# A decoder layer on one core: the delta rule's loop over 64 units written out, five 32 x 32 block transposes on VectorE in each unit in place of PE products, and 24 products of the output projection in the last slot

## The reference

```python
mixed = silu(causal_conv1d(hidden @ w_qkv, conv_w))        # 4 taps
q, k, v = split(mixed)                                     # q, k normalised per head
beta, g = sigmoid(hidden @ w_b), -exp(A_log) * softplus(hidden @ w_a + dt_bias)
def step(St, inp):                                         # for each of 512 tokens
    q_t, k_t, v_t, g_t, b_t = inp
    St = St * exp(g_t)
    delta = (v_t - einsum('bhk,bhkv->bhv', k_t, St)) * b_t
    St = St + k_t[..., None] * delta[:, :, None, :]
    return St, einsum('bhk,bhkv->bhv', q_t, St)
core = rms_norm(core) * norm_weight * silu(hidden @ w_z)
return core.reshape(B, S, 4096) @ w_out                    # 32 heads x 128 -> 512
```

## Time and profile before

| what | us |
|---|---|
| median of 3 runs | 3666.68 |
| the profiled execution | 3667.28 |
| its span, first to last instruction | 3665.5 |
| `delta_rule`, first projection to last `o_turn` | 105.6 to 2802.4 |
| first product of the output projection | 2820.8 |

### The profile page before, as it was taken

One profiled execution on the slowest core, in us unless ns is written; L12 is line 12 of the kernel. 1 busy time (PEld: TensorE's weight loads), 2 busy tenths in 40 slices (PEclk: granted clock), 3 DMA queues, 4 the chain that ended last, 5 costly groups with the idle time before them and its releaser, 6 DMA issues. The chain is left out here.

```text
span 3665.5 us, 67720 instructions
## 1 busy us (share of the span) xinstructions
PE 3487.7 (95%) x23472; PEld 2207.6 (60%) x23472; DVE 2314.8 (63%) x4006; ACT 1369.4 (37%) x4187; POOL 1520.7 (41%) x1473
## 2 busy tenths in 40 slices
PE   4799999999999999999999999999996999999999
PEld 4466666666666666666666666666664444455444
DVE  4587777877778777878778777778772000014453
ACT  1344444444444444444444444444441000011232
POOL 0455554555545455555554555545551000001032
PEclk7999999999999999999999999999997999999999
DMA  1111111111111111111121111111104232311001
GB/s 55 44 36 30 42 42 37 30 36 44 34 36 30 36 32 51 30 36 36 31 48 30 36 30 41 43 37 30 36 24 157 87 115 69 103 58 69 1 9 38
DMA packets 94404, 165.88 MB, mean 45 GB/s; under 512 B 7841, under 2 KB 40737, under 8 KB 92449
## 3 DMA queue, kind: packets, MB, share of 16 engines
q1 hardware_dynamic: 93440, 152.47, 14.4%
q10 hardware_dynamic: 576, 8.39, 0.6%
HBM read 122.83 MB, written 38.01 MB: 44 GB/s over the span
## 5 line engine op out<-in xcount | busy, mean ns | idle before, releaser
L618 PE MATMUL d_ring<-xT,d_w 128*128 128x512 f32 x3072 | 1424.5, 607 | 12.0 <-DMA d_w<-in_w 11.6
L618 PEld LDWEIGHTS d_ring<-xT,d_w 128*128 128x128 f32 x3072 | 574.7, 194 | 585.6 <-issue 567.2
L890 DVE SCALAR_TENSOR_TENSOR d_conv<-d_ring,d_w,d_conv 128x511 f32<-128x511 f32 (+2 forms) x768 | 570.7, 743 | 287.2 <-ACT d_conv L1082 282.4
L1384 PE MATMUL t_acc<-t_area 128*128 128x512 f32 x1024 | 444.8, 595 | 18.4 <-DMA t_area<-core_rows 18.4
L1082 ACT ACTIVATE d_conv<-d_ring,d_w 128x512 f32<-128x512 f32 x256 | 176.5, 689 | 599.3 <-PE d_ring L618 599.3
L1384 PEld LDWEIGHTS t_acc<-t_area 128*128 128x128 f32 x1024 | 194.5, 191 | 256.7 <-issue 237.9
L923 DVE TENSOR_TENSOR d_zm<-d_tz,cons 128x512 f16<-128x512 f32 x384 | 264.2, 688 | 118.9 <-PE d_tz L688 114.5
L559 POOL TENSOR_TENSOR d_imd<-cons,d_dm 128x512 f16<-128x512 f32 x128 | 148.4, 1160 | 434.5 <-ACT d_dm L1133 434.5
L1613 DVE TENSOR_TENSOR t_x<-t_acc,t_x 128x512 f32<-128x512 f32 x16 | 11.1, 692 | 419.5 <-PE t_acc L1384 419.5
L511 POOL TENSOR_TENSOR d_rkt<-d_kss,cons 128x4 f32<-128x4 f32 x64 | 12.9, 201 | 610.9 <-ACT d_junk L1100 610.9
L933 DVE TENSOR_TENSOR d_em<-d_te,d_em 128x512 f16<-128x512 f32 x384 | 262.1, 683 | 4.5 <-PE d_td L697 0.2
(11 more groups left out here) (223 smaller groups left out, 6791.1 us busy)
## 6 DMA issues: line engine op xcount, KB each, us to landing
d_decay<-decay_rows SPq DMA_DIRECT2D x64, 512.0 KB, 6.1
core_rows<-d_core SPq DMA_DIRECT2D x64, 512.0 KB, 3.3
t_area<-core_rows SPq DMA_DIRECT2D x32, 1024.0 KB, 5.5
d_w<-in_w SPq DMA_DIRECT2D x96, 256.0 KB, 2.8
t_area<-in_wout ACTq DMA_DIRECT2D x2, 3072.0 KB, 21.3
ln_x<-in_x SPq DMA_DIRECT2D x16, 256.0 KB, 5.1
t_x<-in_x SPq DMA_DIRECT2D x4, 1024.0 KB, 9.9
t_area<-in_ctx SPq DMA_DIRECT2D x4, 1024.0 KB, 7.5
```

Of the source, the lines that this page charges most:

```text
L618: last = nc.tensor.matmul(bank(TILE[j])[:, :], wtile(j, k), xT[:, k, r % B * S:(r % B + 1) * S], start=k == 0, stop=k == KT - 1)
L890: nc.vector.scalar_tensor_tensor(c[:, d:S], bank(TILE[j])[:, 0:S - d], tap(j, KS - 1 - d), c[:, d:S], ALU.mult, ALU.add).then_inc(taps, 1)
L1384: return nc.tensor.matmul(acc[t][:, :], core[(grp * CHUNKS + q) % 3][:, t, h * P:(h + 1) * P], w[:, head, :], start=head == 0, stop=head = ...
```

## The change

1. **No loop.** `slots` and SP's list write all 66 slots out, and every count to wait for is a constant.
2. **Block transposes on VectorE.** `turn_e0`, `copy_d0` and the levels 0 to 3 of `level_e` go. As the matrices of those levels are block diagonal in blocks of at most 32, `flip_e0` makes the first `dm` and `flip_d` makes `em` after levels 0 to 3, each by one DVE transpose of 128x1024 fp16 in 32 x 32 blocks: 5 in a slot. Levels 4 and 5 keep their `level_e`.
3. **Work between engines.** `normal_k` goes from DVE to ACT (4 pieces of 128x128). `kq` is copied to SBUF by ACT (`copy_kq`) and multiplied by POOL (`p_full`, 2 a slot), no longer by DVE (L916). `first_state` and `first_output` (L952, L964) go from DVE to ACT. The order of all four lists and the ring's bank plan are new, and v0 comes before v1.
4. **Early products.** The ring and `td` use the four accumulators of the output projection, which now outlive `delta_rule`, as `xT` does. In `delta_rule` SP loads two `core` chunks and two weight chunks of 1 MB each into `xT` once the projections no longer need it. 24 of the 32 products of heads 0 to 7 and sequence 0 stand among the recurrence of the last slot (`head_start`), and 8 at the start of `tail`. `tail` begins its loads with chunk 2, and each piece of weights but the first waits for a chunk of `core`.

The core of the diff; the lists of the slots are shown by rows further down:

```diff
         def slots(eng, slot):
-            for r in range(ROUND):
-                slot((0, r), True, r >= 1, r >= 2)
-            with eng.Fori(1, ROUNDS, 1) as q:
-                for r in range(ROUND):
-                    slot((q, r), True, True, True)
-            slot((ROUNDS, 0), False, True, True)
-            slot((ROUNDS, 1), False, False, True)
+            for u in range(ITERS + 2):
+                slot((u // ROUND, u % ROUND), u < ITERS, 1 <= u <= ITERS, u >= 2)
...
+            sp.wait_ge(z_projected, GV * (ITERS - 1))
+            sp.wait_ge(stored, 16 * (ITERS - 4))
+            for q, b in ((0, 1), (1, 0)):
+                sp.dma_start(xT[:, :, b * S:(b + 1) * S], core_rows[0:NC, :, q * S:(q + 1) * S].rearrange("t p n -> p t n")).then_inc(early[0], 16)
+            sp.dma_start(xT[:, :, 2 * S:3 * S], wout[:, 0:KT, :]).then_inc(early[0], 16)
             slot((ROUNDS, 0), False, True, True)
+            sp.wait_ge(z_projected, GV * ITERS)
+            sp.dma_start(xT[:, :, 3 * S:4 * S], wout[:, KT:2 * KT, :]).then_inc(early[1], 16)
...
+            def p_full(m, h):
+                pool.wait_ge(kqs_ready, count(m))
+                pool.wait_ge(gamc_ready, nth(m, "gamc_ready", h))
+                nc.gpsimd.tensor_tensor(pT[m[1] % 2][h][:, :], kqs[:, :], gamc[m[1] % 2][h][:, :], ALU.mult).then_inc(p_ready, 1)
...
-            def turn_e0(m, h):
...
-                for c in range(NC):
-                    last = nc.tensor.matmul(chunk((tz, td)[h], c), piece(em[m[1] % 2], h, c), id16[:, :], start=True, stop=True)
...
+            def head_start(n, i):
+                if isinstance(n[0], int) and n == (ROUNDS, 1):
+                    if i == 0:
+                        pe.wait_ge(early[0], 48)
...
+                    for piece in range(EARLY * i // 19, EARLY * (i + 1) // 19):
+                        if piece == 4 * KT:
+                            pe.wait_ge(early[1], 16)
+                        early_product(nc, acc, xT, piece)
...
+            def flip_e0(m):
+                dve.wait_ge(e0_ready, at(m, 2 * GV, 2 * GV))
+                nc.vector.transpose(dm[:, :], em[m[1] % 2][:, :]).then_inc(flipped, 1)
+
+            def flip_d(m, l):
+                dve.wait_ge(d_added, at(m, 4, l + 1))
+                nc.vector.transpose(em[m[1] % 2][:, :], dm[:, :]).then_inc(flipped, 1)
...
+            def normal_k(n):
+                act.wait_ge(k_turned, count(n))
+                act.wait_ge(rk_ready, at(n, 2, 2))
...
+                for c in range(NC):
+                    nc.scalar.activation(chunk(khat[n[1] % 2], c), chunk(bank("k_turn"), c), ACT.Copy, scale=rk[:, c:c + 1]).then_inc(khat_ready, 1)
+
+            def copy_kq(m):
+                act.wait_ge(kq_done, count(m))
+                wait(act, p_ready, at(back(m, 1), GV, GV))
+                nc.scalar.activation(kqs[:, :], bank("kq")[:, :], ACT.Copy).then_inc(kqs_ready, 1)
...
+            for piece in range(EARLY, 8 * KT):
+                early_product(nc, acc, xT, piece)
             for grp in range(B):
-                for q in range(CHUNKS - 2):
+                for q in range(0 if grp else 2, CHUNKS - 2):
                     out_chunk(grp, q)
...
-        PARTS = (0, 2, 8, 20, HV)
+        PARTS = (8, 12, 16, 24, HV)
...
             for i in range(4):
+                if i:
+                    act.wait_ge(core_loaded[i - 1], 16)
                 act.dma_start(w[:, PARTS[i]:PARTS[i + 1], :], a["wout"][:, PARTS[i]:PARTS[i + 1], :]).then_inc(w_loaded[i], 16)
```

More of the change, by code:

```diff
@@ L424, in conv_of, with free @@
             return cb[CONV_BUFFER[name]]
-        def free(eng, n, name, order, place, freed):
-            slot_, v = back(n, -(name in LAGGED)), order.index(name)
+        def free(eng, n, name, order, place, freed, lag):
+            slot_, v = back(n, -lag[name]), order.index(name)
             for _ in range(3 * len(order)):
@@ L871, in slot @@
                 if recur:
+                    solve(s, 3)
+                    head_start(n, 15)
+                if invert:
+                    level_z(m, 5)
+                    v_turn(m, 1)
+                if recur:
+                    attend(s, 3)
+                    head_start(n, 16)
+                if invert:
+                    level_d(m, 5)
+                    level_e(m, 5)
+                if project:
+                    tile(n, 3)
+                if invert:
+                    refine(m, 1)
+                    refine(m, 0)
+                    tile(m, 4)
+                    close(m, 0)
+                if recur:
+                    o_turn(s, 0)
+                    head_start(n, 17)
                     o_turn(s, 1)
+                    head_start(n, 18)
                 if invert:
-                    close(m, 0)
                     close(m, 1)
+                    v_turn(m, 0)
             slots(pe, slot)
@@ L1227, with early_product, early_weights, tail @@
 A_X, A_H, A_HH, A_RES = (10752, 11776, 12800, 26624), 16384, (0, 2560, 5120, 18432), 20992
-def tail(nc, a, cons):
+def early_product(nc, acc, xT, piece):
+    head, t = piece // 4, piece % 4
+    core = xT[:, t, (1 - head // 4) * S + head % 4 * P:(1 - head // 4) * S + (head % 4 + 1) * P]
+    return nc.tensor.matmul(acc[t][:, :], core, early_weights(xT, head), start=head == 0, stop=False)
+def early_weights(xT, head):
+    return xT[:, head % 4, (2 + head // 4) * S:(3 + head // 4) * S]
+def tail(nc, a, cons, xT, acc, early):
     with ExitStack() as ctx:
@@ L1383, in project_out @@
                 head = q * 4 + h
-                return nc.tensor.matmul(acc[t][:, :], core[(grp * CHUNKS + q) % 3][:, t, h * P:(h + 1) * P], w[:, head, :],
+                rhs = early_weights(xT, head) if head < 2 * KT else w[:, head, :]
+                return nc.tensor.matmul(acc[t][:, :], core[(grp * CHUNKS + q - 2) % 3][:, t, h * P:(h + 1) * P], rhs,
                                         start=head == 0, stop=head == HV - 1)
@@ L1926, in decoder_layer @@
             gate_tables(nc, xT, tabs, cons, a["wab"], a["dt"], a["alog"], a["decay_rows"])
-            delta_rule(nc, xT, tabs, cons, nw, a["decay"], a["w"], a["core"])
-        tail(nc, a, cons)
+            acc = [outer.enter_context(nc.psum_tensor(f"acc{i}", [P, S], F32)) for i in range(4)]
+            delta_rule(nc, xT, tabs, cons, nw, acc, early, a["decay"], a["w"], a["core"], a["core_rows"], a["wout"])
+        tail(nc, a, cons, xT, acc, early)
 def lay_out(i):
```

477 lines of the change are left out of this document (232 added, 245 removed).

## The result

| | before | changed |
|---|---|---|
| median of the runs, us | 3667.24 (3666.51 to 3670.01, 4 runs) | 3456.73 (3456.25 to 3459.3, 4 runs) |
| ratio, 95% interval | 1 | 0.9426 (0.941 to 0.9442) |
| span of the profiled execution, us | 3665.5 | 3455.3 |

The kernel is 210.5 us faster where I had forecast 188.

A forecast was written before the change was run, and what follows sets the result against it. PE's issue of products was taken as the bound: 3665.5 - 86 (products) - 85.6 (loop) - 24 (end) + 8 (handoffs) = 3478 us of span, forecast 3479 us. Its own range was 3460 to 3505, the wider range 3455 to 3535.

The forecast's parts named there:

- What bounds it: In straight slots PE's issue of products is the bound, busy in all of 40.13 us; everything else is hidden.
- The slot: Four levels of e and two turns leave PE, 1.36 us in each of 63 slots: 86 us gained.
- The handoffs: Late answers stall PE at z and d of levels 1, 4 and 5: 0.12 us a slot, 8 us lost.
- VectorE: Five transposes a slot at 1.2 us each; DVE at 32.4 us, POOL 24.9, ACT 21, none passing PE.
- The loop: Writing out all slots removes the stall of 6.1 us at each of 14 returns: 85.6 us gained.
- The end: Early products and loads gain 34.9 us in the tail, lengthen the last slot by 11: net 24 us.
- cold start: At the tail's start PE begins at half clock, costing 2.6 us beside 6.9 us for the 8 products left.
- The rule on the ports: If transposes lock POOL out of the shared port, 3542 us follows; if not, the summed forecast stands.
- Late handoffs: Rival: handoffs through POOL late by 1 us a slot, PE stalling at z: 3542 us; chance 0.15.
- products that give nothing back: Rival: the early products' gain is lost in the last slot's chain or the tail's wait: 3503 us; chance 0.08.
- starved straight code: Rival: straight code starves PE of instructions as often as the branch did: 3565 us; chance 0.04.
- transposes as the bound: Rival: from 3.1 us a transpose DVE makes the kernel slower; at 3.5 us, 3800 us; chance 0.03.

The follow-up runs named there:

- e_ghost: Changed kernel with the removed PE groups put back as five idle copies a slot, each beside an fp16 group: 3545.62 us, slot 39.96.
- e_ghost2: Changed kernel with five idle product groups a slot, four of them between fp32 groups, not beside fp16: 3564.64 us, slot 40.28.
- e_flips2: Changed kernel with each of the five block transposes a slot on VectorE made twice: 3640.13 us, ratio 0.993.
- e_turn_first: Changed kernel with `khat_turn` moved ahead of attend 1 and `q_turn` ahead of read_q 3: 3511.49 us, ratio 0.9581.
- e_turn_last: Changed kernel with `k_turn` moved behind read_q 1 and `v_turn(m, 1)` behind attend 3: 3513.16 us, ratio 0.9587.
- e_early0: Changed kernel with early loads kept but all 32 early products made at the tail's start, none in the last slot: 3467.73 us, ratio 0.9464.

## Why the prediction was right, and where its numbers were off

*What bounds it.* Right: PE's issue in all slots, before and after; putting 1.36 us of products back costs 1.39 a slot (`e_ghost`).

*The slot, the mis-sized term.* I had 1.36 us less a slot, 1.56 came (97 us over 62 slots, in place of 86 over 63). The products were rightly priced (1.39 in `e_ghost`). What I left out is that the rest of PE's instructions don't keep their price when they are put in another order. An fp32 product group costs 0.08 us more behind an fp16 group than behind fp32, a transpose 0.03 or nothing. In a slot before, 15 product groups stood behind fp16 (four tiles, eleven small ones), in one of the changed kernel 11, with two transposes at 0.47 and one `attend` behind such a transpose at 0.48: 4 x 0.08 less 3 x 0.03 is 0.23, for 0.17 to 0.20 found (1.56 less 1.39 or 1.36). `e_ghost2` made four such places and got 0.32. It could have been read beforehand: 0.53 at 238.94, 0.44 for the same kind of group behind fp32 (at 219.25 in the same trace), and the order of both kernels says how many there are.

*The handoffs.* I took 8 us; they cost nothing. The walk through the new lists found only a part of the tight places (it named levels 1, 4 and 5; `e_flips2` waits at levels 2 and 3, and `e_turn_first` and `e_turn_last` at banks that come free just in time) and was too careful in giving each a price. This term and the one above are both off to the same side, 11 + 8 us, and make up nearly all of the 22 between forecast and result; the end gave 2 more than forecast, and the slot of the last inversion, for which I had counted nothing, 1. These errors add up and don't cancel; the forecast's own range was missed by 3 us.

*VectorE.* The transpose takes 1.24 us where I took 1.2 by the slope of 256 to 512 columns; VectorE has 32.97 us a slot for 32.4, POOL 24.4 for 24.9, ACT 20.6 for 21.

*The loop.* 85.6 us predicted, 85 and 84 measured from two sides. I put the 6.1 us of a return to the loop and not to the handoff that the trace named; the runs bear it out. The tile of 5.38 us that I had counted in it is the lower clock behind the stall (0.70).

*The end.* Predicted +11 us for the last slot and -34.9 for the tail. From the first `solve` to the loads' issue went 27.43 us before (2779.10 to 2806.53) and go 37.81 now, +10.4; from there to product 33 44.4 and 7.93, -36.5. Net 26 for 24. The 2.6 us of cold start that I had put into the tail did not come: its 8 products took 7.11 us at a granted clock of 1.00 (2632.87 to 2640.00). The low clock came ahead of them, behind the wait of 4.35 us in the last slot. The loads took 7.88 us for the 7 that I had estimated.

*The rule on the ports.* The Trainium skill, page "SBUF — State Buffer", section "SBUF: two separate sides", lets a VectorE instruction with two SBUF inputs (against a POOL instruction that reads SBUF) or in a 2-port mode lock POOL out. Of the two outcomes worked out ahead, the sum stood: the transpose has one input and leaves POOL at 1.04 and 1.16 us, also twice over. The trace agrees for the scan, as before: POOL's copy takes 1.15 us beside it and 0.22 without it.

*The rivals.* Late handoffs (3542), products that give nothing back (3503), starved straight code (3565) and transposes as the bound (3800) are all refuted: the first by the slot of 38.57, the second by `e_early0`, the third by the absence of any wait in 62 slots, and the fourth by the 1.24 us of a transpose. `e_flips2` shows that the fourth was nearer than my threshold of 3.1 us a transpose: at 2.5, where I had VectorE just full and `no room for a handoff`, nearly all of the gain is gone (0.993), since the handoffs are late before the engine is full.

## What to carry to other kernels

When one engine's issue is the bound, price every one of its groups by what stands ahead of it: on PE, count the places where an fp32 product follows an fp16 one, and when products must be inserted, put fp16 beside fp16. Room on a second engine is to be read at each handoff, not from its busy share: one more microsecond on VectorE cost 0.13 us at the one place and 0.44 on the mean of five, though the engine was idle for 15% of the slot. Work that is to hide in another phase goes where the engine waits, a piece for each wait by its length; spread evenly it lengthens the chain.

## What the runs showed of the hardware

A block transpose of 128 x 1024 fp16 elements on VectorE takes 1.24 us, 1.16 from its start to that of the instruction behind it (209.68 to 210.84; 1.27 where the second transpose of `e_flips2` waits for the first), and does not slow POOL. An fp32 product group of PE costs 0.07 to 0.09 us more directly behind an fp16 group of 64-column products (0.52 against 0.44 to 0.45 for four products of 128 columns, and 3.51 against 3.43 for the eight instructions of a tile, so it does not grow with the size). Behind fp16 groups of 128 columns a tile takes 3.48 or 3.49, 0.05 to 0.06 more, and behind fp16 a transpose takes 0.44 to 0.47. Why, no run shows. A hardware loop's return costs a full PE 4.3 to 7.3 us (28 returns in two kernels), the lower clock behind it included, and the trace books it under another releaser in each of them. Behind a wait of 4.35 us PE's next product of 512 columns took 1.7 us for 0.86; windows of the changed kernel ahead of the wait and behind it:

```profile
2615.00:2619.78 4.78, 4.78 (x19) 2.79 (x19) 0.61 (x2) 1.59 (x7) 0.00 (x0) 1.00 0.00 0
2625.16:2628.50 3.34, 3.34 (x10) 2.20 (x11) 0.75 (x1) 0.00 (x0) 0.00 (x0) 0.53 0.00 0
```

The granted clock is 1.00 before (2.4 GHz) and 0.53 behind it, nearly all at the lower level of 1.2 GHz.
